# Quarter-wide softmax denominators spread by DMA, and a reordered end of the state space stage

## The chip, the core and the metric

One NeuronCore of one Trainium2 chip runs the whole program in one launch. The metric is device time in microseconds (us), from launch to end, the median of three runs; lower is better. The core's engines run side by side and meet at semaphores: PE (TensorE, matmuls; PEld is its weight loading), DVE (VectorE), ACT (ScalarE), POOL (GpSimd) and SP (SyncE, which here issues all DMAs).

## The reference

A block of four layers on x of 2 x 1024 tokens of width 128, each added to x, each fed by a layernorm:

```python
x = x + attention(norm(x))     # 16 heads of 64, causal, v = k
x = x + mixture(norm(x))       # 16 experts of 64, top 2, and a shared one
x = x + state_space(norm(x))   # conv of 3 taps, scan over time, gate
x = x + mixture(norm(x))       # the same weights

# attention, each head
attn = softmax(where(causal, q @ k.T / 8, -max))
out = attn @ k

# the end of state_space
y = (y - mu) * rsqrt(var + 1e-5)
y = y @ W_si + b_si
y = y + D * x_main
y = y * sigmoid(gate)
out = y @ W_out + b_out
```

## The kernel before

Attention comes first (`attention`). Heads are worked in pairs; a pair of one batch row is a unit, and there are `UNITS` = 16 of them. A unit's two heads are l = 0 and 1. Scores are laid out transposed (keys on partitions, queries along the free axis), so the softmax sum of a query runs over partitions. ACT writes exponentials into `probs`; POOL adds the slots of a unit up into `sums` (`add_up`, eleven steps; the first half of the queries is ready after step 4, the second after step 11); PE's `denominators(g, half)` multiplies `sums` by a column block of ones, which sums over partitions and leaves a copy of the sum on 64 partitions for each head. That is one matmul for each head: 128 rows of contraction, 64 output columns, 512 queries. Head 0 lands on partitions 0 to 63 of the PSUM bank `misc`, head 1 on 64 to 127. ACT's `invert` takes Ln and Exp(-x) of the bank into `inv[half]`; DVE's `scale_out` multiplies the outputs in the bank `out_ps` by `inv[half]`. PE's `outputs(g, r)` of the next round waits for that multiplication, since both halves use one bank.

Every engine's order is written out by hand. A unit runs through five rounds (`ROUNDS`), in which PE mixes the scores of this unit, the row maxima of the next, the outputs of the one before. `denominators(unit, 0)` stands in round 3 of the unit, `denominators(unit - 1, 1)` in round 1 of the next one. Both stand behind `outputs` (L643, tiles of 128 rows by 64 columns) and ahead of `scores` (L616, tiles of 64 rows by 128 columns). `scale_out(unit - 1, 0)` stands in DVE's round 0 of the next unit, `scale_out(unit - 1, 1)` in round 4. SP loads the query and key weights of each pair (`load_w`), then the output weights. `turn_max` uses the bank `misc` too.

`state_space` is the third layer. At its end PE has written four output tiles (`outputs(1)`, L1383); DVE adds each to `z` in SBUF (`add_out`, L1548); the sums are multiplied by the gates `sg`, two by POOL (L1308) and two by DVE (`multiply`, L1555); then DVE computes the layernorm of the first group of tokens (`first.norm`, L758 and L96). The block ends when every engine has come to its end. The next block is the second `mixture`. There PE makes twelve 128-column passes of the state space's last matmul (`ssm_out`, L1672), then transposes the normalized first group (L780); ACT and DVE split it in a high and a low part (L774, L765), and the router's logits, the choice of experts and the first spread of weights (`spread`, L1111) follow.

Of the kernel before, what the change touches and what calls it, by code (L numbers as in the profile page):

```python
# [217 lines left out]
NSUM = len(SUM_NEEDS)  # L218
HALF_SUMS = [4, NSUM]
SUMMED_AT = [1, 2, 5, 4, 4, 6, 7, 8, 10]  # L220

# [17 lines left out]
def attention(nc, k, w_qk, load_x, load_w_out):  # L239
# [3 lines left out]
    with Scope(nc, "at") as s:  # L243
# [9 lines left out]
        w_lo = [s.sb(f"w_lo{i}", [P, 2, P], F32R) for i in range(2)]  # L253
        inv = [s.sb(f"inv{h}", [P, BANK]) for h in range(2)]
        half_max = s.sb("half_max", [P, 2, QT, 2])
        row_max = s.sb("row_max", [P, 2, DH])
# [16 lines left out]
        scores_ready, exp_done, av_done, summed = s.sem("scores_ready"), s.sem("exp_done"), s.sem("av_done"), s.sem("summed_up")  # L273
        den_ready, ln_done, inv_done, out_used = s.sem("den_ready"), s.sem("ln_done"), s.sem("inv_done"), s.sem("out_used")

        wq_view = w_qk.rearrange("d (a c) -> d a c", a=2)

        def rows(l):

            return slice(DH * l, DH * l + DH)  # L280

        def pair(what, unit, n=0):
# [74 lines left out]
        with nc.Block() as block:  # L357
            @block.sync
            def _(sp):
                for p in range(1, PAIRS):  # L360
                    load_w(sp, p)
                sp.wait_ge(knat_ps_ready, UNITS)
                sp.wait_ge(k_low, UNITS)
                load_w_out(sp)

            @block.gpsimd
            def _(pool):
                def add_up(unit, n):

                    pool.wait_ge(exp_done, NSLOT * unit + SUM_NEEDS[n] + 1)  # L370
                    if unit and n == 0:
                        pool.wait_ge(den_ready, 2 * (2 * unit - 1))
                    if unit and n == HALF_SUMS[0]:
                        pool.wait_ge(den_ready, 2 * (2 * unit))
                    wait(pool, summed, NSUM * unit + n)
# [39 lines left out]
            def _(act):  # L415
# [23 lines left out]
                def invert(g, half):  # L439

                    n = 2 * g + half
                    act.wait_ge(den_ready, 2 * n + 2)
                    wait(act, out_used, n - 1)
                    act.activation(inv[half][:, :], misc[:, :], ACT.Ln).then_inc(ln_done, 1)  # L444
                    act.wait_ge(ln_done, n + 1)
                    act.activation(inv[half][:, :], inv[half][:, :], ACT.Exp, scale=-1.0).then_inc(inv_done, 1)

# [33 lines left out]
            def _(dve):  # L481
# [34 lines left out]
                def scale_out(g, half):  # L516

                    dve.wait_ge(inv_done, 2 * g + half + 1)
                    dve.wait_ge(av_done, 2 * (NBURST * g + (NBURST if half else 1)))
# [38 lines left out]
            def _(pe):  # L558
# [90 lines left out]
                def denominators(g, half):  # L649

                    pe.wait_ge(summed, NSUM * g + HALF_SUMS[half])
                    if half:
                        pe.wait_ge(rows_done, min(g + 2, UNITS))
                    wait(pe, ln_done, 2 * g + half)
                    for l in range(2):
                        pe.matmul(misc[rows(l), :], ones[:, :], sums[:, l, half * BANK:(half + 1) * BANK],  # L656
                                  start=True, stop=True).then_inc(den_ready, 1)

# [125 lines left out]
def mixture(nc, tag, k, f, source, source_ready=None, load_x=None, weights=None, next_norm=False, store=None, ahead_of=None, first=None):  # L784
# [9 lines left out]
    with Scope(nc, tag) as s:  # L794
# [39 lines left out]
        def interleave(pieces, emit, step, tiles=False):  # L834

            todo = [item for item in agenda(pieces, next_norm, tiles)
                    if item[2] >= early or item[1] not in ("source", "statistics", "root", "norm")]
            for g in range(-1, NSTEPS):
# [308 lines left out]
class StateSpaceWeights:  # L1147
# [69 lines left out]
    [("gate", i) for i in range(2, 2 * SETS)] + [("out", SETS + i) for i in range(2, SETS)]  # L1217
SSM_BANKS = 4


def state_space(nc, k, v, z, source, first):
# [5 lines left out]
    with Scope(nc, "ss") as s:  # L1227
# [64 lines left out]
        with nc.Block() as block:  # L1292
            @block.gpsimd
            def _(pool):
# [4 lines left out]
                for i in range(2 * SETS):  # L1299
# [3 lines left out]
                                       b_si[:, c:c + 1], ALU.mult, ALU.add).then_inc(skipped, 1)  # L1303
                for i in (1, 3, SETS, SETS + 2):
                    h, b, c = out_tile(i)
                    pool.wait_ge(closed, i + 1)
                    pool.wait_ge(gate_done, SETS * (h + 1))
# [3 lines left out]
            def _(pe):  # L1311
# [65 lines left out]
                def outputs(half_of):  # L1377
                    pe.wait_ge(yt_done, half_of + 1)
                    for i in range(SETS * half_of, SETS * (half_of + 1)):
# [4 lines left out]
                                  start=True, stop=True).then_inc(out_ready, 1)  # L1384

                def first_source():
                    pe.wait_ge(first_z, KT)
# [26 lines left out]
                gate(2 * SETS - 1)  # L1414
                outputs(1)

            @block.scalar
# [61 lines left out]
            def _(dve):  # L1479
# [62 lines left out]

                def add_out(i):
# [4 lines left out]
                    dve.tensor_tensor(z[c][:, r], z[c][:, r], bank("out", i)[:, :], ALU.add).then_inc(closed, 1)  # L1548

                def multiply(i, gates):  # L1550
                    h, b, c = out_tile(i)
                    r = tokens(b, h)
                    dve.wait_ge(closed, i + 1)
                    dve.wait_ge(gate_done, gates)
                    return dve.tensor_tensor(z[c][:, r], z[c][:, r], sg[c][:, r], ALU.mult)  # L1555

# [140 lines left out]
```

## Time and profile before

| | us |
|---|---|
| median of three runs | 796.08 (795.87 to 797.96) |
| the profiled execution | 797.62 |
| its span, first to last instruction | 795.8 |
| PE busy | 738.3 |
| DVE, ACT, POOL busy | 455.8, 386.8, 429.4 |

Attention takes the span from about 20 to 501 us, the first mixture to about 640, the state space layer to 684, the second mixture the rest. The profile gives busy time by engine, the granted TensorE clock (PEclk: 1.00 is 2.4 GHz, 0.50 is 1.2 GHz), groups of instructions by line, waits with what released them, and a timeline. A timeline line reads: start, duration, engine, line, operation, output<-inputs, tile shape (rows*columns of the array for PE), operand sizes, xcount, and in brackets the idle time ahead with its releaser. Neighbouring like instructions are merged into one line with a count. Each fp32 matmul of the program shows as two records, one for each of its two passes through the array.

### The profile page before, as it was taken

How to read it: one execution, taken by the hardware profiler on the slowest of the kernel's cores; microseconds unless marked ns; L12 is line 12 of the kernel's file. 1: busy time of each engine (PE TensorE's matmuls, PEld its weight loads, DVE VectorE, ACT ScalarE, POOL GpSimd, SP SyncE). 2: the span in 40 equal slices, each digit the busy share in tenths (PEclk: the TensorE clock that was granted, in tenths of full speed). 3: DMA queues.
4: the chain of work that ended last, by engine and by line, in shares of the span. 5: the costliest groups of instructions: out<-in, count | busy, mean ns of one | idle time of the engine just before them, and what ended most of it. 6: DMA issues, size and time to landing. Idle time of an engine off the chain costs nothing. (4 is left out here: it accounts for less than half of the span.)

```text
span 795.8 us, 14382 instructions
## 1 busy us (share of the span) xinstructions
PE 738.3 (93%) x5520; PEld 499.9 (63%) x5520; DVE 455.8 (57%) x1216; ACT 386.8 (49%) x476; POOL 429.4 (54%) x311
## 2 busy tenths in 40 slices
PE   2789999999999999999999998999989999689998
PEld 1456556555655655655655554887878875468887
DVE  5765665665565675565566540257565547665542
ACT  2355546545555555554654544235753543465421
POOL 3346865765675685685676568015455331345443
PEclk9699999999999999999999999999999999799999
DMA  2000000000000000000000000733233000033232
GB/s 66 7 2 1 2 8 1 7 2 1 8 2 1 8 1 1 8 2 1 1 2 1 28 1 1 174 80 100 77 93 92 17 1 0 2 109 105 92 99 80
DMA packets 29752, 25.56 MB, mean 32 GB/s; under 512 B 10162, under 2 KB 21236, under 8 KB 29684
## 3 DMA queue, kind: packets, MB, share of 16 engines
q1 hardware_dynamic: 29684, 24.64, 10.6%
q8 instruction: 44, 0.72, 0.4%
q14 instruction: 24, 0.20, 0.1%
HBM read 23.32 MB, written 1.31 MB: 31 GB/s over the span
## 5 line engine op out<-in xcount | busy, mean ns | idle before, releaser
L378 POOL TENSOR_TENSOR all_x<-all_x,at_probs 128x1024 f32<-128x1024 f32 (+3 forms) x128 | 221.9, 1733 | 35.7 <-ACT at_probs L453 21.0
L453 ACT ACTIVATE at_probs<-at_ring 128x1024 f32<-128x1024 f32 x144 | 147.2, 1023 | 114.1 <-PE at_ring L625 107.3
L498 DVE CUSTOM_DVE_ANT_0 at_ring<-at_ring,at_after_query 128x128 f32<-128x128 f32 (+3 forms) x256 | 119.5, 520 | 74.4 <-PE at_ring L590 74.4
L643 PE MATMUL at_out<-at_probs,at_k_nat 128*64 128x512 f32 (+3 forms) x768 | 140.3, 494 | 1.1 <-DVE a_attn_t L521 0.9
L1091 POOL TENSOR_TENSOR m_prod<-m_gate,m_wb 128x512 f32<-128x512 f32 x64 | 83.0, 1304 | 97.7 <-ACT m_gate L946 93.6
L378 POOL TENSOR_TENSOR all_x<-at_probs 128x768 f32<-128x768 f32 (+1 forms) x32 | 67.1, 2095 | 126.7 <-ACT at_probs L453 126.6
L643 PEld LDWEIGHTS at_out<-at_probs,at_k_nat 128*64 128x64 f32 x768 | 49.2, 136 | 69.9 <-issue 66.0
L494 DVE TENSOR_REDUCE at_half_max<-at_ring 128x2 f32<-128x1024 f32 x64 | 75.4, 1221 | 12.2 <-PE at_ring L590 12.2
L1000 DVE TENSOR_TENSOR m_hid<-m_prod,m_u 128x512 f32<-128x512 f32 x64 | 43.4, 685 | 66.4 <-POOL m_prod L1091 66.2
L616 PE MATMUL at_ring<-at_qh,at_kh 64*128 64x512 f32 (+3 forms) x384 | 73.6, 380 | 6.2 <-DVE at_m_rows L512 2.6
L866 PEld LDWEIGHTS m_acc<-rest_wd,m_hid 128*128 128x128 f32 x576 | 74.7, 191 | 5.9
L625 PE MATMUL at_ring<-at_m_rows,at_ones_r 64*128 64x512 f32 (+3 forms) x384 | 76.0, 392 | 0.0
L866 PE MATMUL m_acc<-rest_wd,m_hid 128*128 128x128 f32 x576 | 75.2, 275 | 0.0
L946 ACT ACTIVATE m_gate<-m_g 128x512 f32<-128x512 f32 x72 | 42.6, 598 | 66.3 <-PE m_g L858 65.0
L590 PE MATMUL at_ring<-at_kh,at_qh 64*128 64x512 f32 (+3 forms) x384 | 65.5, 390 | 8.5 <-DVE at_half_max L498 2.4
L616 PEld LDWEIGHTS at_ring<-at_qh,at_kh 64*128 64x128 f32 x384 | 36.5, 187 | 52.8 <-issue 37.2
L618 PE MATMUL at_ring<-at_ql,at_kh 64*128 64x512 f32 (+3 forms) x384 | 67.0, 345 | 0.0
L620 PE MATMUL at_ring<-at_qh,at_kl 64*128 64x512 f32 (+3 forms) x384 | 66.9, 344 | 0.0
L590 PEld LDWEIGHTS at_ring<-at_kh,at_qh 64*128 64x128 f32 x384 | 36.4, 190 | 29.3 <-issue 26.0
L485 DVE TENSOR_TENSOR at_ql<-at_ring,at_qh 128x1024 fp32r<-128x1024 f32 x16 | 19.6, 1225 | 55.5 <-ACT at_qh L429 55.5
L444 ACT ACTIVATE at_inv<-at_misc 128x512 f32<-128x512 f32 x32 | 19.1, 598 | 65.3 <-PE at_misc L656 65.3
L620 PEld LDWEIGHTS at_ring<-at_qh,at_kl 64*128 64x128 f32 x384 | 36.4, 186 | 4.3
(234 smaller groups left out, 1284.1 us busy)
## 6 DMA issues: line engine op xcount, KB each, us to landing
m_wb<-m_wt_far SPq DMA_DIRECT2D x128, 128.0 KB, 3.0
all_x<-in_L_attn_a_x SPq DMA_DIRECT2D x8, 256.0 KB, 3.8
at_w_raw<-in_L_attn_a_W_qk SPq DMA_DIRECT2D x8, 128.0 KB, 2.5
out<-all_x SPq DMA_DIRECT2D x4, 256.0 KB, 3.0
a_room<-in_L_attn_a_W_out SPq DMA_DIRECT2D x1, 512.0 KB, 3.9
m_raw_wg<-in_L_ffn_experts_wg SPq DMA_DIRECT2D x1, 512.0 KB, 4.6
m_raw_wu<-in_L_ffn_experts_wu SPq DMA_DIRECT2D x1, 512.0 KB, 4.2
rest_wd<-in_L_ffn_experts_wd SPq DMA_DIRECT2D x1, 512.0 KB, 4.2
```

The lines of the kernel that those rows point to most:

```text
L378: return pool.tensor_tensor(sums[:, :, a * P:b * P], left, right, ALU.add)
L453: act.activation(probs[:, :, slot * BANK:(slot + 1) * BANK], pair("S", unit, slot)[:, :, :], ACT.Exp, scale=BETA).then_inc(exp_done, 1)
L494: last = dve.reduce_max(half_max[:, :, i, out], pair("M", unit, m)[:, :, at:at + w], AX.X)
L498: last = dve.tensor_tensor_reduce(out=sums_ps, in0=sums_ps, in1=after_query[:, BANK - w:BANK], scale=1.0, scalar=MASKED, op0=ALU.add, op1= ...
L590: last = pe.matmul(out[:, l, at:at + (b - a) * P], qh[u][rows(l), i * P:(i + 1) * P], kh[u][rows(l), a * P:b * P], start=True, stop=True)
L616: pe.matmul(to[l], kh[u][rows(l), keys], qh[u][rows(l), q], start=True, stop=False)
L618: pe.matmul(to[l], kh[u][rows(l), keys], ql[u][rows(l), q], start=False, stop=False)
L620: pe.matmul(to[l], kl[u][rows(l), keys], qh[u][rows(l), q], start=False, stop=False)
L625: last = pe.matmul(to[l], ones_r[rows(l), :], m_rows[u][rows(l), q], start=False, stop=True)
L643: last = pe.matmul(out_ps[rows(l), o:o + (b - a) * P], k_nat[g % 3][:, j, rows(l)], probs[:, l, at:at + (b - a) * P], start=(j == 0), stop ...
L866: last = pe.matmul(acc[:, t * P:(t + 1) * P], hid[g % BUFS][:, t * P:(t + 1) * P], f.wd[:, st, :], start=(st == 0 and t == 0), stop=(st == ...
L1091: pool.tensor_tensor(prod[g % BUFS][:, :], gate[g % BUFS][:, :], wb[q % SPREAD][:, :], ALU.mult)\
```

## The change

In attention, for all units but the last, each head's 512 queries of a half are cut in two pieces of 256, and each piece is summed by a matmul with 32 columns of ones. The four results lie on the four quarters of the partitions, in the first 256 columns of `misc`. ACT inverts 128 x 256 into a new tile `inv_q[half]` in place of 128 x 512. Since each inverse now stands on 32 partitions and not on 64, SP copies the pieces with eight DMAs of 32 partitions x 1 KB each into `inv[half]`, and DVE's `scale_out` waits for their 8 x 16 counts. The last unit keeps the wide form, with no DMA. SP's loads of weights are interleaved with these copies in an order by units; the counts on which POOL waits (`dens`) follow the number of matmuls.

In the state space layer's last part DVE adds the output tiles in another order, first the two that POOL multiplies. The sums of the two that DVE itself multiplies are left in their PSUM banks, and its multiplications read them there. PE makes thirteen passes of 128 x 512 after its last output, into a bank that nobody reads. `first.norm` moves from the end of that block to the start of DVE's work in the second mixture.

```diff
@@ attention @@
+                def spread(g, half):
+                    n, w = 2 * g + half, BANK // 2
+                    sp.wait_ge(inv_done, n + 1)
+                    wait(sp, out_used, n - 1)
+                    for l in range(2):
+                        for c in range(2):
+                            for d in range(2):
+                                sp.dma_start(inv[half][quarter(l, d), c * w:(c + 1) * w], inv_q[half][quarter(l, c), :])\
+                                  .then_inc(inv_spread[half], 16)
+                load_w(sp, 1)
+                for unit in range(UNITS):
+                    if unit % 2 == 0 and unit // 2 + 2 < PAIRS:
+                        load_w(sp, unit // 2 + 2)
+                    if unit:
+                        spread(unit - 1, 1)
+                    if unit < UNITS - 1:
+                        spread(unit, 0)
...
-                    act.wait_ge(den_ready, 2 * n + 2)
-                    wait(act, out_used, n - 1)
-                    act.activation(inv[half][:, :], misc[:, :], ACT.Ln).then_inc(ln_done, 1)
+                    act.wait_ge(den_ready, dens(g, half + 1))
+                    wait(act, inv_spread[half], SPREADS * 16 * g)
+                    if g < UNITS - 1:
+                        to, den = inv_q[half][:, :], misc[:, 0:BANK // 2]
+                    else:
+                        to, den = inv[half][:, :], misc[:, :]
+                        wait(act, out_used, n - 1)
+                    act.activation(to, den, ACT.Ln).then_inc(ln_done, 1)
...
-                    dve.wait_ge(inv_done, 2 * g + half + 1)
+                    if g < UNITS - 1:
+                        dve.wait_ge(inv_spread[half], SPREADS * 16 * (g + 1))
...
+                        for c in range(2):
+                            at = half * BANK + c * BANK // 2
+                            pe.matmul(misc[quarter(l, c), 0:BANK // 2], ones[:, 0:DH // 2], sums[:, l, at:at + BANK // 2],
+                                      start=True, stop=True).then_inc(den_ready, 1)
@@ mixture @@
-                    if item[2] >= early or item[1] not in ("source", "statistics", "root", "norm")]
+                    if item[2] >= early or item[1] not in ("source", "statistics", "root")]
@@ state_space @@
-                for i in (1, 3, SETS, SETS + 2):
+                for i, n in ((1, 2), (3, 4), (SETS, SETS + 1), (SETS + 2, SETS + 2)):
...
+                def busy(n):
+                    for _ in range(n):
+                        pe.matmul(turn_ps[:, :], v.w_hi[:, TAPS, 0:P], k.xhi[:, 0:BANK], start=True, stop=True)
...
                 outputs(1)
+                busy(WARM)
...
-                for i in range(SETS, 2 * SETS):
+                for i in (SETS, SETS + 2):
                     add_out(i)
                 for i in (SETS + 1, SETS + 3):
-                    multiply(i, 2 * SETS)
-                first.norm(dve, 0, first_x)
+                    add_out(i, bank("out", i)[:, :])
+                for i in (SETS + 1, SETS + 3):
+                    multiply(i, 2 * SETS, bank("out", i)[:, :], 2 * SETS)
```

## Rows read from the trace of the kernel before

**Rows 1.** The page: busy time by engine, and granted TensorE clock in 40 slices

```profile
PE 738.3 (93%) x5520; PEld 499.9 (63%) x5520; DVE 455.8 (57%) x1216; ACT 386.8 (49%) x476; POOL 429.4 (54%) x311
PEclk9699999999999999999999999999999999799999
```

**Rows 2.** Windows, one unit: length, then PE, PEld, DVE, ACT, POOL busy, clock

```profile
102.00:130.80 28.80, 28.37 (x242) 16.61 (x240) 17.61 (x43) 15.62 (x18) 18.68 (x11) 1.00 0.00 1
```

**Rows 3.** PE's waits from 100 to 450 us: total, times, longest

```profile
PE at_ring L616 <- DVE at_half_max L498: 1.3, 8, 0.2
```

**Rows 4.** L656, the denominators: duration min/median/max in ns, first and last start

```profile
L656 PE MATMUL at_misc<-all_x,at_ones x128: 592/592/644, 54.4 to 495.4; 128*64 128x512 f32 x128
```

**Rows 5.** Timeline of PE around denominators, unit 6, and the last ones

```profile
226.74 1.03 PE L656 MATMUL at_misc<-all_x,at_ones 128*64 128x512 f32 x4
227.17 0.60 PE L656 MATMUL at_misc<-all_x,at_ones 128*64 128x512 f32 x2
227.70 0.50 PE L616 MATMUL at_ring<-at_qh,at_kh 64*128 64x512 f32 x2
...
494.94 1.08 PE L656 MATMUL at_misc<-all_x,at_ones 128*64 128x512 f32 x4 [1.69 <-POOL all_x L378]
```

**Rows 6.** Timeline of PE around an output burst between two changes of tile shape

```profile
220.47 0.39 PE L590 MATMUL at_ring<-at_kh,at_qh 64*128 64x512 f32 x2
220.79 1.08 PE L643 MATMUL at_out<-at_probs,at_k_nat 128*64 128x512 f32 x4
221.80 0.50 PE L616 MATMUL at_ring<-at_qh,at_kh 64*128 64x512 f32 x2
```

**Rows 7.** Groups by shape, 60 to 520 us: busy, mean ns; and a timeline line

```profile
L643 PE MATMUL at_out<-at_probs,at_k_nat 128*64 128x512 f32 x384 | 98.9, 609 | 1.1 <-DVE a_attn_t L521 0.9 <-issue 0.2
L643 PE MATMUL at_out<-at_probs,at_k_nat 128*64 128x256 f32 x128 | 19.3, 379 | 0.0
...
240.46 0.71 PE L578 MATMUL at_ring<-all_ident,a_room 64*128 64x64 f32 x16
```

**Rows 8.** Timeline: inverse of unit 6, half 0, and the multiplication with it

```profile
228.47 0.63 ACT L446 ACTIVATE at_inv<-at_inv 128x512 f32<-128x512 f32 x1
...
241.15 0.69 DVE L521 TENSOR_TENSOR a_attn_t<-at_out,at_inv 128x512 f32<-128x512 f32 x1
```

**Rows 9.** SP's weight spreads in the mixtures: issue in ns, and time to landing

```profile
L1111 SPq DMA_DIRECT2D m_wb<-m_wt_far x128: 444/596/1582, 528.5 to 780.9; - x128
...
DMA to landing us min/median/max: 2.6/3.0/4.0
```

**Rows 10.** Timeline from the last outputs of the state space to the second mixture

```profile
677.55 1.31 PE L1383 MATMUL ss_ring<-ss_yt,rest_w_si 64*128 64x512 f32 x4
...
680.74 1.75 DVE L1555 TENSOR_TENSOR m2w_z<-m2w_z,a_attn_t 128x512 f32<-128x512 f32 x1
682.62 1.11 DVE L96 TENSOR_SCALAR m2w_first_xn<-all_x,m2w_first_moments,m2w_first_rstd 128x128 f32<-128x128 f32 x4
684.06 2.90 PE L1672 MATMUL m_g<-rest_w_out,m2w_z 128*128 128x128 f32 x12 [5.20 <-PEq L1292]
686.75 0.96 PE L780 MATMUL m_misc<-all_ident,m2w_first_xn 128*128 128x128 f32 x4
...
687.75 0.60 ACT L774 ACTIVATE all_xhi<-m_misc 128x512 fp32r<-128x512 f32 x1 [6.00 <-PE m_misc L780]
```

**Rows 11.** Windows, PE alone: length, busy, clock, DMA share; full and half clock

```profile
684.06:686.75 2.69, 2.69 (x12) 0.50 0.03 6
...
501.48:513.95 12.47, 12.47 (x111) 1.00 0.89 222
694.36:697.80 3.44, 3.44 (x19) 0.51 0.04 10
```

**Rows 12.** L1548, the additions from PSUM, and L1308, POOL's products: min/median/max ns

```profile
L1548 DVE TENSOR_TENSOR m2w_z<-m2w_z,ss_ring x6: 678/680/682, 661.2 to 679.5; 128x512 f32<-128x512 f32 x6
...
L1308 POOL TENSOR_TENSOR m2w_z<-m2w_z,a_attn_t x4: 1262/1279/1739, 675.2 to 680.2; 128x512 f32<-128x512 f32 x4
```

More of the change, by code:

```diff
@@ L219 @@
 HALF_SUMS = [4, NSUM]
+SPREADS = 8
 SUMMED_AT = [1, 2, 5, 4, 4, 6, 7, 8, 10]
@@ L254, in attention @@
         inv = [s.sb(f"inv{h}", [P, BANK]) for h in range(2)]
+        inv_q = [s.sb(f"inv_q{h}", [P, BANK // 2]) for h in range(2)]
         half_max = s.sb("half_max", [P, 2, QT, 2])
@@ L274, in attention @@
         den_ready, ln_done, inv_done, out_used = s.sem("den_ready"), s.sem("ln_done"), s.sem("inv_done"), s.sem("out_used")
+        inv_spread = [s.sem(f"inv_spread{h}") for h in range(2)]
         wq_view = w_qk.rearrange("d (a c) -> d a c", a=2)
@@ L280, in rows, with dens, quarter @@
             return slice(DH * l, DH * l + DH)
+        def dens(g, halves):
+            return 4 * (2 * g + halves) - (2 * halves if g == UNITS - 1 else 0)
+        def quarter(l, c):
+            return slice(DH * l + DH // 2 * c, DH * l + DH // 2 * (c + 1))
         def pair(what, unit, n=0):
@@ L359, in _ @@
             def _(sp):
-                for p in range(1, PAIRS):
-                    load_w(sp, p)
+                def spread(g, half):
[15 more added lines that the diff above has]
+                        spread(unit, 0)
                 sp.wait_ge(knat_ps_ready, UNITS)
@@ L371, in add_up @@
                     if unit and n == 0:
-                        pool.wait_ge(den_ready, 2 * (2 * unit - 1))
+                        pool.wait_ge(den_ready, dens(unit - 1, 1))
                     if unit and n == HALF_SUMS[0]:
-                        pool.wait_ge(den_ready, 2 * (2 * unit))
+                        pool.wait_ge(den_ready, dens(unit - 1, 2))
                     wait(pool, summed, NSUM * unit + n)
@@ L441, in invert @@
                     n = 2 * g + half
-                    act.wait_ge(den_ready, 2 * n + 2)
-                    wait(act, out_used, n - 1)
-                    act.activation(inv[half][:, :], misc[:, :], ACT.Ln).then_inc(ln_done, 1)
+                    act.wait_ge(den_ready, dens(g, half + 1))
[6 more added lines that the diff above has]
+                    act.activation(to, den, ACT.Ln).then_inc(ln_done, 1)
                     act.wait_ge(ln_done, n + 1)
-                    act.activation(inv[half][:, :], inv[half][:, :], ACT.Exp, scale=-1.0).then_inc(inv_done, 1)
+                    act.activation(to, to, ACT.Exp, scale=-1.0).then_inc(inv_done, 1)
                 def exponentials(unit, slot):
@@ L516, in scale_out @@
                 def scale_out(g, half):
-                    dve.wait_ge(inv_done, 2 * g + half + 1)
+                    if g < UNITS - 1:
+                        dve.wait_ge(inv_spread[half], SPREADS * 16 * (g + 1))
+                    else:
+                        dve.wait_ge(inv_done, 2 * g + half + 1)
                     dve.wait_ge(av_done, 2 * (NBURST * g + (NBURST if half else 1)))
@@ L655, in denominators @@
                     for l in range(2):
-                        pe.matmul(misc[rows(l), :], ones[:, :], sums[:, l, half * BANK:(half + 1) * BANK],
-                                  start=True, stop=True).then_inc(den_ready, 1)
+                        if g == UNITS - 1:
+                            pe.matmul(misc[rows(l), :], ones[:, :], sums[:, l, half * BANK:(half + 1) * BANK],
+                                      start=True, stop=True).then_inc(den_ready, 1)
+                            continue
+                        for c in range(2):
+                            at = half * BANK + c * BANK // 2
+                            pe.matmul(misc[quarter(l, c), 0:BANK // 2], ones[:, 0:DH // 2], sums[:, l, at:at + BANK // 2],
+                                      start=True, stop=True).then_inc(den_ready, 1)
                 project(0, "K")
@@ L1218 @@
 SSM_BANKS = 4
+WARM = 13
 def state_space(nc, k, v, z, source, first):
@@ L1303, in _ @@
                                        b_si[:, c:c + 1], ALU.mult, ALU.add).then_inc(skipped, 1)
-                for i in (1, 3, SETS, SETS + 2):
+                for i, n in ((1, 2), (3, 4), (SETS, SETS + 1), (SETS + 2, SETS + 2)):
                     h, b, c = out_tile(i)
-                    pool.wait_ge(closed, i + 1)
+                    pool.wait_ge(closed, n)
                     pool.wait_ge(gate_done, SETS * (h + 1))
@@ L1541, in norm, with add_out @@
                        .then_inc(normed, 1)
-                def add_out(i):
+                def add_out(i, to=None):
                     h, b, c = out_tile(i)
@@ L1547, in add_out, with multiply @@
                     dve.wait_ge(skipped, SETS * (h + 1))
-                    dve.tensor_tensor(z[c][:, r], z[c][:, r], bank("out", i)[:, :], ALU.add).then_inc(closed, 1)
-                def multiply(i, gates):
+                    dve.tensor_tensor(z[c][:, r] if to is None else to, z[c][:, r], bank("out", i)[:, :], ALU.add)\
+                       .then_inc(closed, 1)
+                def multiply(i, gates, added_up=None, sums=0):
                     h, b, c = out_tile(i)
                     r = tokens(b, h)
-                    dve.wait_ge(closed, i + 1)
+                    dve.wait_ge(closed, sums or i + 1)
                     dve.wait_ge(gate_done, gates)
-                    return dve.tensor_tensor(z[c][:, r], z[c][:, r], sg[c][:, r], ALU.mult)
+                    return dve.tensor_tensor(z[c][:, r], z[c][:, r] if added_up is None else added_up, sg[c][:, r], ALU.mult)
                 late.statistics(dve, 0, last_x)
```

## Prediction

> **What bounds the kernel now.** I read the shares of busy time first, then windows of single units, then PE's waits, and last the timeline at the places that the change touches. PE is busy 738.3 of 795.8 us, the next engine 455.8 [rows 1]. In one unit of attention PE is busy 28.37 of 28.80 us, while DVE, ACT and POOL have at most 18.68 [rows 2]. From 100 to 450 us the largest of PE's waits adds up to 1.3 us, in eight pieces of at most 0.2 [rows 3]. So up to the last units attention is the sum of what PE does, and time taken from PE comes off the span. At the end POOL leads: PE idles 1.69 us for its sums before the last denominators [rows 5]. Between state space and second mixture PE does nothing from 678.86 to 684.06 us, and its clock has fallen: 0.50 in the work after it [rows 10, 11]. That stretch is a chain over several engines.
>
> **Denominators.** A pair (two heads, two passes each) stands as four records. The two heads' records start together, the second passes 0.43 us after the first (226.74, 227.17), and the next matmul starts at 227.70: 0.96 us a group [rows 5]. Records of 512 and 256 elements last 609 and 379 ns, 0.23 us apart, so a pass over 256 takes about half of 0.43, 0.215 us [rows 7]. The last stage of the group is 0.53 and not 0.43 us, since the next work has another tile shape (64*128): 0.10 us for a change of shape [rows 5]. The isolated burst of L643 between two such changes takes 1.01 us from start to next start, 0.86 for its two stages plus 0.15: 0.10 at the exit and 0.05 for first weights that nothing hides; L656's longest record is 52 ns over its median as well [rows 4, 6].
>
> With quarters, a half has four tiles, eight records of 256. If the four work at once, as the two do now, the group is two stages of 0.215, 0.43 us, plus 0.10 at the exit. The entry is new: L643 ahead of it has tiles of 64 columns, and now they become 32. No row shows a change from 64 to 32 columns with rows unchanged. Its bounds are nothing (the present entry) and 0.15 us (the entry and exit of rows 6). I take 0.15, because those rows are changes of the column width too. So 0.68 against 0.96: 0.28 us saved; at the other end 0.43. Weights for twice as many records don't bind: L578 passes sixteen records of 64 elements in 0.71 us, of which 0.22 are the last one's own length, so about 35 ns each against four in 215 ns [rows 7].
>
> Thirty halves become quarters (15 units). The first has scores ahead of it, a change of shape that is paid already: 0.43. The half 1 of unit 14 comes when POOL leads the end, and I count it as nothing. 28 x 0.28 + 0.43 = 8.3 us; with the cheap entry 29 x 0.43 = 12.5.
>
> The Trainium skill speaks against the edit here. Its page TensorEngine Tiling (Array Packing), Key Properties, says that a change of tiling mode drains the array. The 0.10 us at each exit agree with it [rows 5, 6]; by that rule the sum is the 8.3, without it the 12.5.
>
> **Inverses and spreads.** ACT's Ln and Exp shrink; ACT has 13 us of room in each unit [rows 2], so this is worth nothing. `scale_out` now waits for DMAs. An inverse ends at 228.47 + 0.63 = 229.10, its multiplication starts at 241.15: 12.0 us of room [rows 8]. For half 1 there is more (round 1 to round 4). The nearest DMAs issue in 0.60 us each and land 3.0 us later, 4.0 at most [rows 9]; eight take 4.8 to 5.1 us with gaps, 9 with the slowest landing. They fit by 3 us, and cost nothing. Were they late, `scale_out` would be late, behind it on DVE the low part of the queries, and PE at `outputs(g, 1)`. SP's `load_w` stand ahead of a spread and wait for POOL's split at the head of a unit, before the denominators whose inverse the spread carries; nothing is behind them. The output weights load a unit later, with some 20 us before their use. The counts for POOL name the same events.
>
> **The end of the state space.** DVE's second product takes 1.75 us while POOL's takes 1.74, against 1.26 for POOL's shortest and 0.68 for additions with one operand in PSUM, which run beside POOL as well [rows 10, 12]. With sums in PSUM I take 0.69 for each: the additions end at 679.5 + 0.68 = 680.2 [rows 12], and DVE at 680.2 + 0.1 + 1.4 = 681.7, and POOL near 681.6. No row shows both an addition into PSUM and a product out of it; the ends are 0.68 and 1.75 each. The layernorm (682.42 to 683.73, 1.31 us) goes behind the block's end. PE's thirteen passes begin at 677.55 + 1.31 = 678.86; at full clock they are 0.23 us apart as the 512-element matmuls of this precision (0.32 with a change of shape at 220.47 [rows 6]): 3.0 us, to 681.9, 682.1 with the last one's drain. So PE is the last by a little. The gap from the old end (683.73) to PE's start (684.06) is 0.33: new start 682.4.
>
> From there two things run side by side: the layernorm, to 682.4 + 1.3 + 0.1 = 683.8, and PE's twelve records of L1672. They took 2.69 us at clock 0.50; at 1.00 the same work takes 12.47 / 111 = 0.112 each, 1.35 us, and some 0.2 to start: 684.0 [rows 11]. L780 then starts at 684.0 in place of 686.75, 2.75 us earlier, and its four records are done 0.36 us sooner at full clock (about 0.64 to ACT's start in place of 1.00 [rows 10]). Sum 3.1 us. Logits, choice of experts and first spread hang on it one after another, so it is passed on. The extreme where the passes run at 0.50 all the same is 13 x 0.43 = 5.5 us, to 684.4: start 684.7, L780 at 687.5, a loss of 0.75. On the good side is another 1.7 us: from 694.36 to 697.80 PE works at half clock again [rows 11], behind a stretch in which it waits for the choice of experts. Whether this stretch is found cold again, with all shifted by 12 us, I can't say; I count nothing.
>
> **Sum.** 8.3 + 3.1 = 11.4 us. The profiled execution has 797.62, 1.5 above the median; its span is 795.8. 797.6 - 11.4 = 786.2 there, and 796.08 - 11.4 = 784.7 at the median. A measurement of this kernel can tell 0.3%, 2.4 us, from no change.
>
> **Rivals.**
> A, the forecast: four column tiles at once. For it: two tiles start within the same hundredth of a microsecond now, in two stages and not four [rows 5]. Own range from 796.1 - 12.5 - 3.1 - 1.7 = 778.8 to 788.5 (7 from attention, 0.6 from the tail). 0.80.
> B, slower: the quarter tiles go one after another. Four streams of 128 partitions would have to be fed at once, where the trace shows two. Eight stages of 0.215 and 0.25 for the shapes are 1.97 us, 1.01 more than now in each of 29 halves: 29 - 3.1 = 26 slower, 822. It decides from a group of 0.96 + 3.1 / 29 = 1.07 us on. Against it: today's overlap. 0.05.
> C, two at a time: four stages, 0.86 + 0.25 = 1.11 us, 0.15 more; 29 x 0.15 = 4.4, less 3.1: 797.4. 0.08.
> D, something between: the feeds slow each other, a group near 0.85, 29 x 0.11 = 3.2 plus 3.1: 789.8. 0.04.
> E, the spreads are late: half 0 needs over 12 us from inverse to landing. At 1.5 us for each DMA in SP it would be 12 + 4 = 16, 4 us in each of 15 units: 60 slower less 11, 845. Against it: 0.60 us issues. 0.03.
>
> The skill has a rule that would make A smaller. TensorE: Matmul & The Clock Gate, Measured speedup vs the span model, gives 2.38 times for three column tiles of 512, not 3; no run here shows such an isolated pack. By that share of 79%, as an estimate, two stages of 0.27 would leave 0.17 us a half, and the time would be about 788, inside A's range.
>
> **How the numbers follow.** The likeliest case gives 784.7. Faster by over 0.3%: A and D, 0.84. Within: C, 0.08. Slower: B and E, 0.08. A and D together hold 0.84, from 778.5 to 790, and their outer parts little: that is the range.
>
> **What would show it.** In the profile of the changed kernel: L656's successor in 32-column tiles with eight records of 256, two starts 0.215 apart, and about 0.68 us to the next shape; units of 28.8 - 0.56 = 28.2 us; `scale_out` following the outputs as now, with no idle on a DMA; PE's clock at 1.00 through the gap; L780 2.7 to 3.2 us nearer to L1383's start than the 9.20 of now. Wrong would be: eight starts spaced evenly, PE waits on DVE's L521 in every unit, or thirteen passes at half clock that end after DVE.

## The result and the profile after

The changed kernel takes 783.41 us (783.19 to 784.04, four runs) against 796.62 for the one before in the same session: a ratio of 0.9837, 95% interval 0.9824 to 0.9849, 13.2 us less. The forecast was 784.7, which is 11.4 us less. Timed again later, beside four other kernels, the same program took 784.96 (784.03 to 785.96) against 796.60: 0.9853, interval 0.9838 to 0.9868, 11.6 less. The two medians differ by 1.5 us; the experiments show one reason, which is part of it. The profiled execution has 783.28 us, its span is 781.5.

The page of the changed kernel, busy time by engine and the clock in 40 slices, to be held against [rows 1]:

```profile
PE 729.7 (93%) x5653; PEld 495.2 (63%) x5653; DVE 458.5 (59%) x1216; ACT 375.6 (48%) x476; POOL 424.4 (54%) x311
...
PEclk9699999999999999999999999999999999999999
```

The slice at 7 near the end is gone. Windows of one unit (length, then PE, PEld, DVE, ACT, POOL busy, clock, DMA share and GB/s), where [rows 2] has 28.8:

```profile
102.00:130.20 28.20, 27.80 (x254) 16.36 (x250) 17.59 (x42) 14.89 (x18) 18.66 (x11) 1.00 0.08 20
```

PE has 0.57 us less to do in a unit 0.6 us shorter; it still leads. (DVE is busy 2.7 us more in all, which is no part of the change: in this execution seven of the low parts of the keys, L326, take 1.80 us and not 1.23, in that of before one did, and in the second profile of the changed program none.) The timeline of PE around one group of denominators, for [rows 5]:

```profile
222.24 0.60 PE L680 MATMUL at_out<-at_probs,at_k_nat 128*64 128x512 f32 x2
...
222.77 0.64 PE L699 MATMUL at_misc<-all_x,at_ones 128*32 128x256 f32 x8
...
223.01 0.40 PE L699 MATMUL at_misc<-all_x,at_ones 128*32 128x256 f32 x4
...
223.34 0.49 PE L653 MATMUL at_ring<-at_qh,at_kh 64*128 64x512 f32 x2
```

Eight records stand in two stages, 222.77 and 223.01, four at once. In the records one by one the four start 7 ns after each other. From the last stage of L680 to the first of L699 are 0.53 us where two stages of L680 are 0.43 apart: the entry costs 0.10. The group then lasts 0.57, together 0.67 us for the 0.96 of before. All thirty groups last 0.57.

The spreads by DMA, SP's issue in ns min/median/max, and time to landing:

```profile
L380 SPq DMA_DIRECT2D at_inv<-at_inv_q x240: 507/591/1889, 55.5 to 469.4; - x120
...
DMA to landing us min/median/max: 1.7/1.8/3.4
```

And the timeline of DVE at the multiplication with the inverse that ended at 224.4:

```profile
237.37 0.68 DVE L558 TENSOR_TENSOR a_attn_t<-at_out,at_inv 128x512 f32<-128x512 f32 x1
```

In that half the eight issues stand 5.3 us from first to last, so the last lands some 7 us after the inverse, and the multiplication comes at 13.0, with no idle on a DMA. Nor does it wait for the outputs: their last records end at 236.15. DVE comes to it straight from the low part of the keys, which stands ahead of it in DVE's own order, as before:

```profile
233.83 2.32 PE L680 MATMUL at_out<-at_probs,at_k_nat 128*64 128x512 f32 x16
...
235.64 1.80 DVE L326 TENSOR_TENSOR at_kl<-a_room,at_kh 128x1024 fp32r<-128x1024 f32 x1 [0.34 <-ACT at_kh L453]
```

So the last DMA lands some 6 us before it is needed.

The end of the state space, timeline, for [rows 10]:

```profile
669.65 3.25 PE L1433 MATMUL ss_turn<-all_xhi,rest_w_hi 128*128 128x512 f32 x13
...
669.84 2.56 POOL L1352 TENSOR_TENSOR m2w_z<-m2w_z,a_attn_t 128x512 f32<-128x512 f32 x2 [1.30 <-ACT a_attn_t L1481]
...
671.39 0.69 DVE L1607 TENSOR_TENSOR m2w_z<-ss_st,a_attn_t 128x512 f32<-128x512 f32 x1
672.00 0.68 DVE L1607 TENSOR_TENSOR m2w_z<-ss_ring,a_attn_t 128x512 f32<-128x512 f32 x1
...
673.20 1.58 PE L1725 MATMUL m_g<-rest_w_out,m2w_z 128*128 128x128 f32 x12 [0.30 <-PEq L1336]
673.41 1.12 DVE L96 TENSOR_SCALAR m2w_first_xn<-all_x,m2w_first_moments,m2w_first_rstd 128x128 f32<-128x128 f32 x4
...
674.62 0.63 PE L823 MATMUL m_misc<-all_ident,m2w_first_xn 128*128 128x128 f32 x4
...
675.28 0.60 ACT L817 ACTIVATE all_xhi<-m_misc 128x512 fp32r<-128x512 f32 x1 [2.67 <-PE m_misc L823]
```

DVE's products take 0.69 and 0.68, POOL's two 2.56 together; the block ends with PE's passes (672.90), and PE is off for 0.3 us and not 5.2. Twelve records take 1.58 us, 2.90 before.

Where the time went, from the starts of the same instructions in both traces (us, after less before). "Last output" is the last record of the state space's output tiles, "logits" the first of the second mixture's router, "second product" POOL's second one there:

| | before | after | difference |
|---|---|---|---|
| first exponentials of unit 1 | 69.72 | 68.79 | -0.94 |
| last exponentials | 488.62 | 479.48 | -9.14 |
| last output | 678.27 | 669.13 | -9.14 |
| logits | 689.12 | 676.66 | -12.47 |
| second product | 704.98 | 690.89 | -14.09 |
| end | 795.83 | 781.49 | -14.34 |

So 9.1 us come in attention, 3.3 from last output to logits, and 1.6 between logits and second product, where nothing was forecast. The two profiled executions are 14.3 us apart and the medians 13.2, because the profiled execution before was 1.0 us above its median.

### The profile page after: what moved, and what is told of

Its sections match the earlier page's. It is cut to its first block and busy times, and to the rows that moved or that the text cites. A ratio compares the mean times of both kernels' runs of the same rounds, so it can differ in the third digit from the quotient of the medians.

```text
span 781.5 us, 14916 instructions
## 1 busy us (share of the span) xinstructions
PE 729.7 (93%) x5653; PEld 495.2 (63%) x5653; DVE 458.5 (59%) x1216; ACT 375.6 (48%) x476; POOL 424.4 (54%) x311
## 5 line engine op out<-in xcount | busy, mean ns | idle before, releaser
L407 POOL TENSOR_TENSOR all_x<-all_x,at_probs 128x1024 f32<-128x1024 f32 (+3 forms) x128 | 215.3, 1682 | 31.8 <-ACT at_probs L487 17.1
L680 PE MATMUL at_out<-at_probs,at_k_nat 128*64 128x512 f32 (+3 forms) x768 | 140.3, 494 | 1.1 <-DVE a_attn_t L558 0.9
L680 PEld LDWEIGHTS at_out<-at_probs,at_k_nat 128*64 128x64 f32 x768 | 49.2, 136 | 70.0 <-issue 66.1
L558 DVE TENSOR_TENSOR a_attn_t<-at_out,at_inv 128x512 f32<-128x512 f32 x32 | 21.8, 682 | 29.9 <-PE at_out L680 29.9
```

Of the source, the lines that this page charges most:

```text
L407: return pool.tensor_tensor(sums[:, :, a * P:b * P], left, right, ALU.add)
L680: last = pe.matmul(out_ps[rows(l), o:o + (b - a) * P], k_nat[g % 3][:, j, rows(l)], probs[:, l, at:at + (b - a) * P], start=(j == 0), stop ...
```

## Experiments

Each is timed against the kernel before in its own session (797.26 in the first, 796.60 in the second, 797.19 in the third). To see places apart, this table gives two distances in each profiled execution, worked out from the starts of those instructions, and the stretches at clock 0.50 after 100 us:

| kernel | median | last output to logits | logits to second product | at 0.50 |
|---|---|---|---|---|
| before | 796.62 | 10.85 | 15.86 | 680.6 to 687.5, 694.3 to 697.7 |
| changed | 783.41 | 7.53 | 14.23 | none |
| attention alone | 787.90 | 10.95 | 14.42 | 673.9 to 680.7 |
| tail alone | 793.76 | 7.53 | 15.86 | 690.9 to 694.3 |
| narrow tiles, long | 801.50 | 10.95 | 14.53 | 687.7 to 694.6 |
| no passes | 785.12 | 7.30 | 15.86 | 681.6 to 685.0 |
| changed, again | 784.96 | 7.53 | 15.87 | 682.1 to 685.5 |
| no passes, again | 784.86 | 8.57 | 14.24 | 674.0 to 677.4 |
| passes in both places | 784.25 | 7.53 | 14.24 | none |
| second place only | 785.44 | 9.02 | 14.56 | 673.1 to 679.9 |
| sixteen spreads | 785.76 | 7.53 | 15.53 | 682.5 to 685.9 |
| sums in SBUF | 785.83 | 8.18 | 15.75 | 683.1 to 686.5 |
| layernorm back | 786.20 | 8.54 | 14.23 | none |
| eleven and six | 783.18 | 7.30 | 14.23 | none |

**The two parts alone.** The edits are the hunks of the diff in `attention`, and all the others. In the text below, the gap is the time without PE work between state space and second mixture, and the late or second stretch is the one at clock 0.50 while the experts are chosen.

> The kernel before with the attention part alone (quarter denominators, inverses of half the width, spreads by DMA); the state space's end is that of before. Theory: the groups of denominators are 0.66 us where they were 0.96, in 28 halves of 0.29 and one of 0.4, so 8.5 us less, about 788 us, and in the gap between state space and second mixture the clock is 0.50 as before. Rival: part of attention's gain comes from the tail's edits only by way of the clock's phase, or the tail's gain is larger than it seems: then this kernel gains under 7 us, over 789.5.

787.90 us (787.26 to 787.98), ratio 0.9883 (0.9866 to 0.9899), 9.4 less: the theory, with 8.5. Attention's exponentials end 8.7 us earlier, and the distance from last output to logits stays as it was, 10.95. Windows of PE alone (length, busy, clock) show the gap's clock as low as before:

```profile
675.00:677.00 2.00, 1.71 (x8) 0.50 0.03 8
677.00:679.00 2.00, 2.00 (x11) 0.50 0.00 0
```

Yet the second stretch at 0.50 is missing here, with not one of the tail's edits in the kernel, and its 1.4 us with it. The 8.5 lies within the interval of the 9.4, which is 8.1 to 10.7 us.

> The kernel before with the state space's end alone (order of additions, sums in PSUM, thirteen passes, layernorm moved). Theory: the logits of the second mixture stand 3.3 us nearer to the state space's last output than before, and PE keeps its clock through the gap: 3.3 us less, and up to 1.7 more if the second stretch at 0.50 (694 to 698 us before) is gone too; 791.7 to 793.3 us. Rival: the second stretch falls by the time at which things happen, not by the passes; unshifted by attention it is then still there, and the gain is 3.3 us, no more.

793.76 us (793.10 to 795.01), 0.9956 (0.9941 to 0.9970), 3.5 less, just above the 791.7 to 793.3 of the theory. Last output to logits is 7.53, to the hundredth that of the whole change, and the second stretch is there. The rival's figure, no more than 3.3, was right: the tail's edits give 3.3 us here, and the second stretch comes in spite of them. That it comes by the time at which things happen, as the rival has it, isn't shown. The ratio of the two parts, 0.9883 x 0.9956 = 0.9840, is that of the whole, 0.9837.

**What the narrow tiles cost.** Quarter tiles over all 512 queries: the same number of stages as before, four tiles in each. The counts that ACT and POOL wait for double with it.

```diff
...
                     for l in range(2):
-                        pe.matmul(misc[rows(l), :], ones[:, :], sums[:, l, half * BANK:(half + 1) * BANK],
-                                  start=True, stop=True).then_inc(den_ready, 1)
+                        for c in range(2):
+                            q = slice(DH * l + DH // 2 * c, DH * l + DH // 2 * (c + 1))
+                            pe.matmul(misc[q, :], ones[:, 0:DH // 2], sums[:, l, half * BANK:(half + 1) * BANK],
+                                      start=True, stop=True).then_inc(den_ready, 1)
```

> The kernel before with each denominators matmul of 64 columns as two of 32 columns over all 512 queries: four tiles, eight records of 512 and the same result in the bank, no DMA, no other change. It measures the price of the entry into 32-column tiles and whether four streams hold their rate. Theory: stages of 0.43 us as with two tiles, and 0.10 us more at the entry; 31 x 0.10 = 3 us slower, about 799.6 us. Rival 1: the entry is free: no change. Rival 2: four streams share a feed and run 12% slower, as the 0.240 us stage in the changed kernel (0.215 expected) could mean: stages of 0.48, 6 us slower. Rival 3: 0.240 is a fixed time for loading four tiles' weights: stages of 0.43 to 0.45.

801.50 us (800.76 to 803.07), 1.0058 (1.0039 to 1.0076): 4.2 slower. The timeline of PE around a group:

```profile
228.14 0.60 PE L643 MATMUL at_out<-at_probs,at_k_nat 128*64 128x512 f32 x2
228.67 1.07 PE L658 MATMUL at_misc<-all_x,at_ones 128*32 128x512 f32 x8
229.66 0.49 PE L616 MATMUL at_ring<-at_qh,at_kh 64*128 64x512 f32 x2
```

Entry 0.53 less 0.43: 0.10 us. The group is 1.00 us for 0.96; its first stage, in the single records, is 0.454, not 0.430. With 256 queries the first stage is 0.240, not 0.215. The surplus is 0.025 us at both lengths, so it is no slower feed (rival 2, which asks for 0.05 here) but a fixed cost of the first stage; that it is the weights of four tiles, as rival 3 has it, fits, and isn't shown. Theory plus rival 3: 31 x (0.10 + 0.04) = 4.3 us; the interval is 3.1 to 6.1. Four streams of fp32 hold their rate. This kernel, too, has none of the tail's edits and no second stretch in its profile (14.53 from logits to second product).

**The room of the spreads.** Sixteen DMAs of 512 bytes a partition in place of eight of 1 KB, with `SPREADS = 16`.

```diff
...
-                                sp.dma_start(inv[half][quarter(l, d), c * w:(c + 1) * w], inv_q[half][quarter(l, c), :])\
-                                  .then_inc(inv_spread[half], 16)
+                                for e in range(2):
+                                    v = w // 2
+                                    sp.dma_start(inv[half][quarter(l, d), c * w + e * v:c * w + (e + 1) * v],
+                                                 inv_q[half][quarter(l, c), e * v:(e + 1) * v])\
+                                      .then_inc(inv_spread[half], 16)
```

> The changed kernel with each half's spread cut in sixteen DMAs of 32 partitions x 512 bytes in place of eight of 1 KB: the same bytes, twice the issues. It asks how much room the spreads have. In the changed kernel SP issues one each 0.63 us, the last lands 1.8 us after; from the inverse to the multiplication there are 13.0 us for half 0. Sixteen need 16 x 0.63 + 1.8 = 11.9 us: theory: still hidden in units 0 to 13; in unit 14, where the room is 10.4 (half 0) and 11.5, up to 1.5 us late, part of it behind POOL, which leads there. 0 to 1.5 us slower. Rival: a landing is slower with twice as many in flight, or SP reaches them late: 1 us late in 14 units would be 14 us slower, and DVE would be seen to wait for a DMA.

785.76 us (783.89 to 786.61), 0.9850 (0.9834 to 0.9865); by medians alone nothing can be told from 784.96. The trace tells it. The exponentials of unit 15 begin at 462.44 against 462.47 in the changed kernel's second profile, so no unit before has lost anything; the last exponentials come at 481.12 against 479.90, 1.2 us later. The two lines of DVE at which it waits longest for a spread are those of unit 14:

```profile
462.80 0.69 DVE L561 TENSOR_TENSOR a_attn_t<-at_out,at_inv 128x512 f32<-128x512 f32 x1 [3.02 <-DMA at_inv<-at_inv_q]
479.41 0.69 DVE L561 TENSOR_TENSOR a_attn_t<-at_out,at_inv 128x512 f32<-128x512 f32 x1 [15.91 <-DMA at_inv<-at_inv_q]
```

(The idle time in brackets is all that DVE had, not the delay.) The time came out as the theory has it, and only unit 14 passed a delay on. But double issues are not well hidden before it. In half 0 of seven of the units 0 to 13 the multiplication starts 0.02 us after the last landing, and in three of them (2, 6 and 10) DVE has idled 0.08 to 0.35 us for it; in the changed kernel 5.1 to 6.2 us lie between the two there. So twice the issues is about the limit in half 0 of every unit, not only of the last.

**The thirteen passes.** `WARM = 0` in place of 13, twice, and between them the changed kernel again.

> The changed kernel without the thirteen passes that nobody reads, all else as changed. Theory: the clock falls in the gap, the twelve records of the next block take 2.7 in place of 1.6 us and the four transposes 0.4 more, so 1.5 us later at the logits, and a second stretch at 0.50 may come back (1.6): 785 to 786.5 us. Rival: the passes buy nothing, since the gap is short now (2.3 in place of 5.2 us) and the clock stays up; PE was the last engine of its block by 0.2 us, so this is 0.2 us faster.

785.12 us (784.67 to 785.81), 0.9850 (0.9834 to 0.9867). The theory failed in its mechanism, though its time came out. The gap is there, but the clock in the records behind it is 1.00:

```profile
672.98 1.58 PE L1725 MATMUL m_g<-rest_w_out,m2w_z 128*128 128x128 f32 x12 [3.26 <-PEq L1336]
```

```profile
681.50:685.00 3.50, 3.50 (x19) 0.51 0.04 9
```

The first is a line of the timeline, the second a window of PE alone (length, busy, clock). The logits are 0.23 us nearer than with passes; the loss came 9 us after the place where the passes had been, while the experts are chosen.

> The changed kernel once more, beside the next three on one chip. In its profile before, the clock never left 1.00 after the start, whereas without the thirteen passes it stayed up in the gap between the blocks too (the first transposes were even 0.2 us earlier) and fell only later, while the experts are chosen. Theory A (luck): whether that later stretch at 0.50 comes is not set by the passes, which lie 9 us ahead of it. Then this run and the one without passes differ by 0.3 us or less in median, in either direction, or their profiles change places. Theory B (the passes hold it): this kernel is 1.2 to 1.6 us faster than the one without passes again.

> The changed kernel without the thirteen passes, once more, on the same chip as the changed one. Theory A: within 0.3 us of it. Theory B: 1.2 to 1.6 us slower, with a stretch at 0.50 in one of the two places in its profile.

784.96 (784.03 to 785.96) with passes, 784.86 (784.39 to 785.16) without: equal, ratios 0.9853 and 0.9852. And the profiles did change places. The kernel that had no stretch at 0.50 now has one, at 682.1; without passes it fell this time in the gap. Timelines, first of the changed kernel again, then of the one without passes again:

```profile
682.78 3.24 PE L1725 MATMUL m_u<-rest_w_out,m2w_z 128*128 128x128 f32 x16
```

```profile
673.51 2.45 PE L1725 MATMUL m_g<-rest_w_out,m2w_z 128*128 128x128 f32 x12 [3.26 <-PEq L1336]
675.76 1.06 PE L823 MATMUL m_misc<-all_ident,m2w_first_xn 128*128 128x128 f32 x4
```

So theory A in its second form: one and the same program has the late stretch in one execution and not in the other. The stretch does not explain all of the 1.5 us between the two medians. An execution of 784.53 us in the second timing has the same mean granted clock, 0.989, as the profiled one of 783.28 in the first; what the rest is, isn't shown. What the passes buy is the first place only: with thirteen of them it was at 1.00 in all seven profiles, without them and with the shorter gap it fell in one of two here and once more in the next pair of experiments. No gain of theirs shows in the two medians that were timed together. What sets the late stretch stays open, and it may not be independent of the gap: in kernels without passes in the second place it came in five of the seven profiles that had held 1.00 through the gap, and in one of the four that had fallen there (that of before). If holding the clock in the gap only moves the fall, the passes would buy little; eleven profiles are too few to tell.

**Passes in the second place as well.** Six more, where PE waits for the choice of experts:

```diff
                     elif piece == "turn_w":
+                        if first and n == 0:
+                            for _ in range(6):
+                                pe.matmul(misc[1][:, :], f.wg_hi[:, 0:2, :].rearrange("p e i -> p (e i)"), k.xhi[:, cols(0)],
+                                          start=True, stop=True)
                         pe.wait_ge(w_ready, n + 1)
```

> The changed kernel with six more passes of 128 x 512 that nobody reads, on PE between its last filler work and the transposes of the first group's expert weights in the second mixture (PE idles 1.7 us there, six passes are 1.4 us). Theory: where the clock falls there, it costs 1.4 us; with the passes it can't, in any execution, so this is as fast as the changed kernel's best executions and up to 1.4 us faster than its slower ones. Rival: the clock holds there by itself in the changed kernel; then this is equal, or 0.1 us slower where a pass delays the transposes.

> As the last one, but without the thirteen passes between the blocks: only the six in the second mixture. Theory: the gap between the blocks is 2.3 to 4 us without them, in some executions the clock falls in it (12 records 1.1 us longer, transposes 0.4), in others not, and then this is 0.2 us faster than with both, since PE is not the last engine of its block. By theory A of the first of these four, it is at or below the changed kernel; by theory B 0 to 1.5 us above.

With both, 784.25 us (783.70 to 784.41), 0.9844 (0.9830 to 0.9857), and no stretch at 0.50. With the second place only, 785.44 (784.78 to 786.28), 0.9857 (0.9842 to 0.9873): the clock fell in the gap and stayed down for 6.8 us, logits at 9.02. This median is 0.5 us above the changed kernel's, where theory A had said at or below; the intervals overlap, so the medians decide nothing here. The runs with both spread over 0.7 us, those of the changed kernel beside them over 1.9. The median with both is 0.7 us below the changed kernel's, inside the intervals. That the second place is held by its passes rests on two profiles with them and the gap held (this one and eleven and six), against four of the six others that have the thirteen passes and not the six, in which it fell. Two profiles in a row without a fall would come by chance about once in nine times at that rate, so this is likely and not shown.

**The other edits of the tail.** Sums back in SBUF, in the new order; and `first.norm` back at the end of the block, with the `mixture` condition of before.

```diff
-                    add_out(i, bank("out", i)[:, :])
+                    add_out(i)
                 for i in (SETS + 1, SETS + 3):
-                    multiply(i, 2 * SETS, bank("out", i)[:, :], 2 * SETS)
+                    multiply(i, 2 * SETS, None, 2 * SETS)
```

> The changed kernel with the two sums that DVE multiplies written to SBUF and read there, as before the change (the order of additions stays the changed one). Theory: DVE's second product runs against POOL's second and both take 1.75 where they took 0.68 and 1.28; DVE ends 1.1 us later, and since PE's passes ended 0.2 us after DVE, the block ends 0.8 to 0.9 us later: logits 0.8 us farther from the last output. Rival: reordering alone has freed them from one another, or the block's end is PE's anyway: no difference.

> The changed kernel with the first group's layernorm back at the end of DVE's work in the state space's block. Theory: DVE ends 1.3 us later, which is 1.1 us later than PE; after the block's end PE's twelve records (1.4 us from the new start) come before the transposes, which the layernorm no longer holds up, and which they held up by nothing before: the logits are 1.1 us later. Rival: the records and the layernorm each take 1.4 us, so what the layernorm costs in the one place it costs in the other, and less PE work in the gap makes the clock fall: 1.1 plus 1.5 us later.

Sums in SBUF: 785.83 us (784.18 to 786.73), last output to logits 8.18, 0.65 more than with PSUM (0.8 expected). DVE's two products, merged, where the changed kernel's two lines are 0.69 and 0.68:

```profile
672.48 2.17 DVE L1607 TENSOR_TENSOR m2w_z<-m2w_z,a_attn_t 128x512 f32<-128x512 f32 x2
```

In the single records they are 1.57 and 0.68, and POOL's two stay at 1.30 each: it is the DVE product that gives way, and the one that began while POOL was at work. It ends 0.55 us after POOL's second one (674.05 and 673.50). In the trace of before the DVE product that took 1.75 ends 0.55 us after POOL's as well (682.50 and 681.95). Both fit a DVE product that waits for POOL's to end; no run tests that by itself. Layernorm back: 786.20 us (785.01 to 786.99), 8.54, 1.01 more (1.1 expected), with the clock at 1.00 in the gap.

**Eleven and six.** Both edits of the passes, with `WARM = 11`.

> The changed kernel with eleven passes in place of thirteen between the blocks and six more in the second mixture, where PE waits for the choice of experts. Theory: PE ends 0.46 us earlier and DVE is last of its block by 0.2 us, so the block ends 0.2 us earlier, and the clock holds in both places: about 784 us, 0.2 less than with thirteen and six, and 0.5 to 0.9 under the changed kernel on the same chip. Rival: with two passes fewer the clock falls in the gap in some executions: median as the changed kernel.

783.18 us (782.21 to 783.98) against 797.19, ratio 0.9823 (0.9810 to 0.9837); logits at 7.30, 0.23 nearer than with thirteen, clock at 1.00 in both places. It is the lowest ratio of the study, 0.14% under the changed kernel's first and 0.30% under its second; its interval overlaps that of the first timing and ends where that of the second begins (0.9837, 0.9838), and the changed kernel was not timed beside it. So it is a candidate and not shown to be faster.

## Why the prediction was right, point by point

**Who leads.** PE leads in attention: 0.29 us less in a group are 0.57 us less in a unit. From the first exponentials of unit 1 to those of unit 15 the trace has 7.9 us and that of the second profile 8.2, where 28 x 0.29 = 8.1. From there to the last exponentials come another 0.25 and 0.29: the half 1 of unit 14, which was counted as nothing, gives its share all the same.

**The group of denominators.** Forecast 0.68 us, measured 0.67: entry 0.10, where 0.15 was taken with the first weights, first stage 0.240 in place of 0.215, last stage with the exit 0.33 for 0.315. So the entry was 0.05 too dear and the stages 0.04 too cheap. That the two nearly cancel is luck. Case A it was, four at once; B, C and D fell with the two stages. The Trainium skill's rule that a change of tiling mode drains the array (TensorEngine Tiling (Array Packing), Key Properties) agrees with the 0.10 us between 64 and 32 columns, which no row of before could show. The Trainium skill's 2.38 times for three column tiles (TensorE: Matmul & The Clock Gate, Measured speedup vs the span model) would by estimate have asked for stages of 0.27. The measurement decides: the first stages are 0.240 and, with 512 queries, 0.454, so four tiles lose 0.025 us once.

**What attention gave beyond 8.3.** 0.94 us by unit 1, where one group of 0.4 was forecast. The other half microsecond is no part of the change: the second profile of the same program has 0.22 there, and other kernels with the same attention have from 1.08 less to 0.54 more. The start of the kernel waits for its inputs and runs partly at 0.50, and differs by this much from one execution to the next.

**The spreads.** Forecast 0.60 us an issue and up to 4.0 to land; 0.63 and 1.8. Nobody waited for them, and the experiment with double issues puts the limit at about twice as many. Case E fell. That `scale_out` follows the outputs was read wrongly, for before too: it follows the low part of the keys on DVE. It cost the forecast nothing.

**The tail.** Forecast 3.1 us, measured 3.3. Its terms, undone one by one: layernorm 1.0, sums in PSUM 0.65. What is left by subtraction, 1.7, is the order of the additions and the clock, less 0.2 for passes that end after DVE; it was not split further, and it is no measure of the passes, without which the same distance was 7.30 in one profile. PE's start came 673.20 less 669.13 = 4.1 us behind the last output, as forecast. The cost of a fall in this gap is 1.3 us in one profile (8.57 against 7.30) and 1.7 in another.

**The second stretch.** It was named, priced at 1.7 us and counted as nothing. It is worth 1.3 to 1.6 us and comes and goes with no edit near it. The first measurement's 13.2 us lie 1.8 above the sum and the second's 11.6 lie 0.2 above; the profiled execution of the first had no such stretch, that of the second had it. So the sum of 11.4 fits a pair of executions that both have the stretch. The 1.8 us of the first measurement lie, as far as its profile shows, in what was counted as nothing and in the start of the kernel; that its median came out on the good side is luck that no edit brought. How often the kernel before has its own second stretch isn't known: it was profiled once, and its executions spread from 795.7 to 798.2. The wrong reading that was near at hand, that the thirteen passes hold the clock through all that follows, was tested and fell.

## What to carry to other kernels

Where PE leads and a reduction over partitions only needs copies of one row, cut the queries and not the copies: narrow column tiles that work at once halve the stages, and the copies can be made by DMA if some 8 us lie between result and use (from the end of the inverse to the last of eight landings it took 6.2 to 8.0 us here). Count the changes of tile shape: here each cost 0.10 us, and the one at the entry ate a quarter of the 0.43 us saved. Before explaining a microsecond at a place where PE waits, profile the same program twice: its clock may fall in one execution and not in the next.

## What the runs showed of the hardware that was not expected

- Four tiles of 128 x 32 columns with fp32 streams start within 20 ns and hold full rate; the first stage is 0.025 us longer, at 256 and 512 elements alike, and the last with its exit 0.014.
- A DVE product of two SBUF operands next to POOL's takes 1.57 us for 0.68, while POOL's own stays at 1.30 in that run; with one operand in PSUM it takes 0.69. In the trace of before, where the two began half a microsecond apart, both were stretched, to 1.75 and 1.74 [rows 10, 12]. In both traces the stretched DVE product ends 0.55 us after POOL's.
- TensorE's granted clock behind a gap of 3.26 us without PE work: 1.00 in one profile (twelve records in 1.58 us), down to 0.50 within them in the next of the same program (2.45 us). The late stretch began behind an idle time of only 1.73 us in the second profile of the changed kernel (at 682.1), while behind 1.74 us in the first the clock stayed at 1.00.
- A DMA from SBUF to SBUF on 32 partitions lands 1.8 us after its issue and SP issues one each 0.63 us, both in the median, whether it moves 1 KB or 512 bytes on each partition (an issue takes 591 ns both times).
